# Both directions of a selective scan as one stage of 256 units instead of two stages of 128

## The chip, the cores and the metric

One core of one Trainium2 chip runs the whole layer in one launch. The metric is the device time of the program in microseconds (us), the median of several runs. One further execution was profiled; all rows below come from it.

## The reference, cut to what matters

The layer takes x as 1024 channels by 4096 pixels in float32. A first part (normalisation, a scan over channels) makes tokens `t`, 4096 of them with 1024 features. The second part is a bidirectional state space block on the normalised tokens. In it only the order of the sequence differs between the directions; each has weights of its own.

```python
def _direction(x_bdl, conv_w, conv_b, xproj_w, dtproj_w, dtproj_b, A_log, Dv):
    xc = depthwise_conv(x_bdl, conv_w, 4 taps, causal) + conv_b       # 2048 channels
    x_dbl = xc @ xproj_w.T                                            # 64 + 16 + 16 columns
    dt = x_dbl[..., :64] @ dtproj_w.T + dtproj_b
    Bm, Cm = x_dbl[..., 64:80], x_dbl[..., 80:]
    xc, dt = clip(xc, -10, 10), clip(dt, 1e-05, 1.0)
    delta = softplus(dt + dtproj_b);  A = -exp(A_log)
    # for each of 2048 channels and 16 states n, over 4096 tokens:
    #   h = exp(delta * A[n]) * h + (delta * xc) * Bm[n];   y += h * Cm[n]
    return y + xc * Dv
xz = (hidden_states @ in_proj_w.T).transpose(0, 2, 1);  x, z = split(xz)
y = (_direction(x, forward weights) + _direction(x[:, :, ::-1], backward weights)[:, ::-1]) * silu(z)
out = y @ out_proj_w.T
```

## The kernel before, in words

**Tiling.** Channels come in 16 blocks of 128 (`DB`), one channel to a partition, tokens in 8 chunks of 512 (`NCH`, `T`). A *unit* is one block of one chunk with its 16 states; `stage_scan` runs 128 units (`NU`), chunk after chunk, and is called twice: first with `rev=True` (tiles named `bwd_...`), then with `rev=False` (`fwd_...`). `flip` reverses the access patterns of the scan in the backward stage. A `Scope` ends with its semaphores cleared and a barrier of all engines.

**One unit, by engine.** For each state n, ScalarE (ACT) computes `da` = exp(delta * A[n]) into one of two PSUM buffers (L1027), VectorE (DVE) scans (L1171) and, for 12 of the 16 states (`VN`), multiplies by C (`weigh`, L1181). GpSimd (POOL) makes `w` = (delta * u) * B for four states at a time (`weigh_b`, L1122) and multiplies the other four states (`PN`) by C (`weigh_c`, L1131). TensorE (PE) transposes and sums the results in `yT` (L927, L894). ACT's order is fixed: at every n a `save` of a state, which waits for a scan (L1006), then `da`, then whatever hangs at that n.

**Work for later units.** Inside unit b, the input of unit a = b + 17 is prepared (`inputs_of`): in the backward stage the input projection (8 matmuls in two halves at n = 0 and 2, `in_step`), in both stages the convolution (4 diagonal matmuls at n = 5, `conv_step`, L822), ACT's `xc_copy` of it at n = 10 (L977), and the x projection (`project_step`). The forward stage reads the x that the backward one stored (`x_pad`) and instead projects z of its own unit (`in_step(b)`, `in_copy` at n = 7). The last 16 units of a stage have no later unit to prepare. The first chunk of a stage is prepared by `before_scan` in a loop ahead of all units, and `between` loads what the first units need.

**The chunk boundary.** B and C of a chunk (16 x 512 each) are a row product of all 16 blocks; they go to DRAM (`store_bc`) and come back to all 128 partitions by broadcast, 4 states at a time (`broadcast(k, c, g)`: c = 0 for B, 1 for C; L680; 1 MB of SBUF each). In the last unit of a chunk (`at == DB - 1`) the SP queue, which issues every DMA in the order of the code, does this: store of B and C; in the forward stage a hold on the last input matmul and then the 2 MB reload of `hn` (L648); store of `y_out`; B groups 0, 1, 2; C 0; B 3; store of `xc`; C 1; store of z. After a hold on all stores so far come the loads for the next units and, in the next unit, C 2 and 3. The backward stage reloads `hn` one unit earlier, since its input projections run 17 units ahead.

Of the kernel before, what the change touches and what calls it, by code (L numbers as in the profile page):

```python
# [9 lines left out]
P = 128  # L10
# [4 lines left out]
KT = C // P  # L15
# [10 lines left out]
G = 4  # L26
# [512 lines left out]
def stage_scan(nc, rev, ident, hnT_d, win_d, wx_d, wdt_d, convp_d, par_d, skip_d,  # L539
               x_pad_d, xc_d, z_d, bc_d, yT_d):  # L540
    name = "bwd" if rev else "fwd"


    first = rev
    with Scope(nc, name) as sc:
# [12 lines left out]
        par, skip = sc.sb("par", [P, DB, 1 + NS]), sc.sb("skip", [P, DB])  # L558
        convp = sc.sb("convp", [P, DB, TAPS + 1])
        prm = sc.sb("prm", [P, DB, NPAR])  # L560
        wdt = sc.sb("wdt", [R, 2, P])
        xc = sc.sb("xc", [P, 2, T])
        state = sc.sb("state", [P, DB * NS])
# [23 lines left out]
        NU = NCH * DB  # L587
# [4 lines left out]
        def t0(k):  # L592

            return (NCH - 1) * T - k * T if rev else k * T

        def col(k):
            return t0(k) + HALO

        def flip(ap):
            return ap[:, ::-1] if rev else ap  # L600

        last_col = 0 if rev else T - 1
# [6 lines left out]
        def state_of(b, n):  # L609
            i = (b % DB) * NS + n  # L610
            return state[:, i:i + 1]

        def decay(b, n):
            return prm[:, b % DB, n:n + 1]

        x_at = 0 if rev else HALO
        tap_at = [HALO - k if rev else k for k in range(TAPS)]
# [10 lines left out]

        POOL_AT = [5, 8, 11, 14]
        SKIP, DT_AT = 11, 13  # L630

        def stores_of(b):
            return 1 + len(inputs_of(b)) * (2 if first else 1) + (0 if first else 1)

        def stored_to(b):

            return (DB * (2 if first else 1) + sum(stores_of(i) for i in range(b + 1))) * LOAD
# [5 lines left out]
        def _(sp):  # L643
            def load_win(s, db):
                sp.dma_start(win[:, s], win_d[ds(db, 1)].rearrange("o p k d -> (o p) k d")).then_inc(win_in[s], LOAD)

            def load_hn(k):
                sp.dma_start(hn[:], hnT_d.rearrange("(k p) t -> p k t", p=P)[:, :, ds(t0(k), T)]  # L648
                             ).then_inc(S["hn_loaded"], LOAD)

            def load_a(s, db, k):

                if first:
                    halo = x[:, s, T:T + HALO]
                    sp.dma_start(halo, x_pad_d[ds(db * P, P), ds(col(k) + T, HALO)]).then_inc(a_in[s], LOAD)
                else:
                    sp.dma_start(x[:, s], x_pad_d[ds(db * P, P), ds(t0(k), T + HALO)]).then_inc(a_in[s], LOAD)
                sp.dma_start(wx[:, s], wx_d[ds(db, 1)].rearrange("o p k -> (o p) k")).then_inc(a_in[s], LOAD)

            def load_p(b):  # L660
                sp.dma_start(wdt[:, b % 2], wdt_d[b % DB]).then_inc(p_in[b % 2], LOAD)
                sp.dma_start(xc[:, b % 2], xc_d[b]).then_inc(p_in[b % 2], LOAD)

            def store_bc(k):

                hold(sp, S["proj_copied"], k + 1, S["passed"])
                sp.dma_start(bc_d[k], proj[R:XO, :]).then_inc(S["bc_stored"], LOAD)

            def broadcast(k, c, g):

                b = k * DB - 1
                if k and c == 0:
                    hold(sp, S["w_done"], b * NS + g * G + G, S["passed"])
                elif k:
# [3 lines left out]
                dst, sem = ((bcast_b, b_loaded), (bcast_c, c_loaded))[c]  # L678
                src = bc_d[k:k + 1, c * NS + g * G:c * NS + (g + 1) * G].rearrange("o n t -> (o n) t")
                sp.dma_start(dst[:, g * G:(g + 1) * G], src.partition_broadcast(P)).then_inc(sem[g], LOAD)  # L680

            def store_x(a):
                if first:
                    hold(sp, S["in_copied"], a + 3, S["passed"])
                    sp.dma_start(x_pad_d[ds(a % DB * P, P), ds(col(a // DB), T)],
                                 x[:, a % 2, x_at:x_at + T]).then_inc(S["stored"], LOAD)

            def store_xc(a):
                hold(sp, S["xc_copied"], a + 3, S["passed"])
                sp.dma_start(xc_d[a], xc_out[:, a % 2]).then_inc(S["stored"], LOAD)  # L690

            def before_scan(j, end=False):

                n = 2 if first else 1
                for s in range(2):
                    if first and not end:
                        hold(sp, S["in_mm"], j * 2 + s + 1, S["passed"])
                        load_win(s, j * 2 + s + 2)
                for s in range(2):
                    db = j * 2 + s  # L700
                    if first:
                        hold(sp, S["in_copied"], db + 3, S["passed"])
                        sp.dma_start(x_pad_d[ds(db * P, P), ds(col(0), T)],
                                     x[:, s, x_at:x_at + T]).then_inc(S["stored"], LOAD)
                    hold(sp, S["xc_copied"], db + 3, S["passed"])
                    sp.dma_start(xc_d[ds(db, 1)].rearrange("o p k -> (o p) k"),
                                 xc_out[:, s]).then_inc(S["stored"], LOAD)
                    hold(sp, S["stored"], j * (2 * n * LOAD) + (s + 1) * n * LOAD, S["passed"])
                    hold(sp, S["proj_mm"], db + 1, S["passed"])

            def between():
# [3 lines left out]
                if first:  # L715
                    for s in range(2):
                        load_win(s, s)
# [3 lines left out]
                if first:  # L721
                    load_hn(1)
                for s in range(2):
                    load_a(s, s, 1)
                if not first:
                    load_hn(0)
                    for s in range(2):
                        load_win(s, s)
# [3 lines left out]
            def unit(b):  # L732
                k, at = b // DB, b % DB
                more = k + 1 < NCH
                if at == 0 and b:
                    broadcast(k, 1, 2)
                    broadcast(k, 1, 3)
# [4 lines left out]
                if at == DB - 1 and more:  # L742
                    store_bc(k + 1)
                    if not first:
# [6 lines left out]
                if at == DB - 1 and more:  # L751
                    hold(sp, S["bc_stored"], (k + 2) * LOAD, S["passed"])
                    for g in range(3):
                        broadcast(k + 1, 0, g)
                for a, _ in inputs_of(b):
                    store_x(a)
                    if first and a % DB == DB - 1 and a + 1 < NU:
# [3 lines left out]
                if at == DB - 1 and more:  # L761
                    broadcast(k + 1, 1, 0)
                    broadcast(k + 1, 0, 3)
                for a, _ in inputs_of(b):
                    store_xc(a)
                if at == DB - 1 and more:
                    broadcast(k + 1, 1, 1)
                if not first:
                    hold(sp, S["in_copied"], b + 3, S["passed"])
                    sp.dma_start(z_d[ds(at * P, P), ds(t0(k), T)], z_out[:, b % 2]).then_inc(S["stored"], LOAD)  # L770

                hold(sp, S["stored"], stored_to(b), S["passed"])
                for a, _ in inputs_of(b):
                    hold(sp, S["proj_mm"], a + 1, S["passed"])
                    if a + 2 < NU:
                        if first:
                            load_win(a % 2, (a + 2) % DB)
                        load_a(a % 2, (a + 2) % DB, (a + 2) // DB)
                if not first and b + 2 < NU:
                    load_win(b % 2, (b + 2) % DB)  # L780

            sp.dma_start(par[:], par_d.rearrange("u p k -> p u k")).then_inc(S["par_loaded"], LOAD)
            sp.dma_start(convp[:], convp_d.rearrange("u p k -> p u k")).then_inc(S["par_loaded"], LOAD)
            if first:
                load_hn(0)
                for s in range(2):
                    load_win(s, s)
            for s in range(2):
                load_a(s, s, 0)
            for db in range(DB):  # L790
                sp.dma_start(skip[:, db:db + 1], skip_d[db]).then_inc(S["skip_loaded"], LOAD)
            with sp.Fori(0, DB // 2 - 1) as j:
                before_scan(j)
                for s in range(2):
                    load_a(s, j * 2 + s + 2, 0)
            before_scan(DB // 2 - 1, end=True)
# [4 lines left out]
            sp.dma_start(yT_d[NU], y_out[:, 1]).then_inc(S["stored"], LOAD)  # L801
# [4 lines left out]
        def _(pe):  # L806
# [13 lines left out]
            def convolution(s, bank=dt_ps[:]):  # L820
# [615 lines left out]
```

## Time and profile before

| | us |
|---|---|
| median of 3 runs (8814.04 to 8827.7) | 8817.02 |
| the profiled execution, own time | 8824.44 |
| its span in the trace | 8822.7 |
| DVE busy in the span | 7549.8 (86%) |
| PE busy | 7257.8 (82%) |
| POOL busy | 6819.9 (77%) |
| ACT busy | 4939.5 (56%) |

Times in the trace count from the start of the span. The backward stage fills about 626 to 4197, the forward one 4199 to 7767. What lies ahead is the first part of the layer, what follows is `stage_out`. A row of the timeline may merge several instructions of one form (x2, x16); its duration is then that of all of them, from the first start to the last end.

### The profile page before, as it was taken

The page shows a single profiled execution, that of the slowest core. Times are in us where ns is not written, and L with a number is a line of the kernel's source. Part 1 is how long each engine was busy: PE and PEld are TensorE (multiplying, and loading weights), DVE is VectorE, ACT ScalarE, POOL GpSimd, SP SyncE. Part 2 cuts the span into 40 slices and gives each one's busy share as a digit, 9 for nine tenths or more (in the row PEclk, how much of TensorE's full clock was granted, in tenths as well). Part 3 has the DMA queues.
Part 4 walks back from the last instruction along what each step waited for, and adds up shares of the span by engine and source line. Part 5 has one row for each costly group of instructions (what it writes and reads, how often), then busy time and mean ns, then how long its engine had stood idle before and what let it go on. Part 6 is the DMA issues. An engine that isn't in the chain of part 4 may idle for free. (4 is left out here: it accounts for less than half of the span.)

```text
span 8822.7 us, 108252 instructions
## 1 busy us (share of the span) xinstructions
PE 7257.8 (82%) x28624; PEld 4150.8 (47%) x28624; DVE 7549.8 (86%) x8367; ACT 4939.5 (56%) x11727; POOL 6819.9 (77%) x3031
## 2 busy tenths in 40 slices
PE   7458888888888888855688888888888887769999
PEld 3243555454555544444255445554555454434444
DVE  7940999999999999999199999999999999944444
ACT  3552666666666666665266666666666665610000
POOL 1211999999999999999299999999999999931110
PEclk9679999999999999966799999999999998879999
DMA  3263231313132313110323232323232322144442
GB/s 86 57 185 129 70 111 65 111 66 111 65 112 66 111 64 112 61 62 18 116 73 120 75 121 77 118 73 119 76 118 77 121 73 102 49 160 137 135 142 80
DMA packets 540929, 843.59 MB, mean 96 GB/s; under 512 B 112592, under 2 KB 260048, under 8 KB 522960
## 3 DMA queue, kind: packets, MB, share of 16 engines
q1 hardware_dynamic: 540368, 837.29, 28.7%
q8 instruction: 207, 3.39, 0.2%
q14 instruction: 354, 2.90, 0.1%
HBM read 583.83 MB, written 253.28 MB: 95 GB/s over the span
## 5 line engine op out<-in xcount | busy, mean ns | idle before, releaser
L1122 POOL TENSOR_TENSOR fwd_w<-fwd_du,fwd_bcast_b 128x2048 f32<-128x2048 f32 x511 | 2315.5, 4544 | 60.2 <-DMA fwd_bcast_b<-bc 60.2
L1122 POOL TENSOR_TENSOR bwd_w<-bwd_du,bwd_bcast_b 128x2048 f32<-128x2048 f32 x511 | 2316.4, 4545 | 4.0 <-DMA bwd_bcast_b<-bc 4.0
L1171 DVE TENSOR_TENSOR_SCAN bwd_h<-bwd_da,bwd_state,bwd_w 128x512 f32<-128x512 f32 x1536 | 1927.3, 1326 | 21.3 <-issue 14.0
L1171 DVE TENSOR_TENSOR_SCAN fwd_h<-fwd_da,fwd_state,fwd_w 128x512 f32<-128x512 f32 x1536 | 1921.0, 1318 | 26.0 <-POOL fwd_w L1122 10.6
L927 PE MATMUL bwd_yT<-all_ident,bwd_hc 128*128 128x128 f32 x6144 | 1021.6, 305 | 574.0 <-DVE bwd_hc L1181 566.1
L927 PE MATMUL fwd_yT<-all_ident,fwd_hc 128*128 128x128 f32 x6144 | 1000.4, 301 | 494.7 <-DVE fwd_hc L1181 486.7
L1027 ACT ACTIVATE fwd_da<-fwd_delta,fwd_prm 128x512 f32<-128x512 f32 x2048 | 1402.2, 685 | 0.0
L1027 ACT ACTIVATE bwd_da<-bwd_delta,bwd_prm 128x512 f32<-128x512 f32 x2048 | 1402.0, 685 | 0.0
L927 PEld LDWEIGHTS bwd_yT<-all_ident,bwd_hc 128*128 128x128 f32 x6144 | 748.2, 153 | 1061.5 <-DVE bwd_hc L1181 949.3
L927 PEld LDWEIGHTS fwd_yT<-all_ident,fwd_hc 128*128 128x128 f32 x6144 | 734.6, 151 | 985.4 <-DVE fwd_hc L1181 863.3
L1181 DVE TENSOR_TENSOR bwd_hc<-bwd_h,bwd_bcast_c 128x512 f32<-128x512 f32 x1536 | 1011.3, 726 | 16.7 <-ACT bwd_state L1006 16.7
L1181 DVE TENSOR_TENSOR fwd_hc<-fwd_h,fwd_bcast_c 128x512 f32<-128x512 f32 x1536 | 1005.5, 718 | 16.3 <-ACT fwd_state L1006 16.3
L816 PE MATMUL fwd_in_ps<-fwd_hn,fwd_win 128*128 128x512 f32 x2048 | 944.0, 604 | 16.8 <-DMA fwd_win<-winz 16.8
L1317 PE MATMUL out_o_ps<-out_yg,out_wout 128*128 128x512 f32 x2048 | 890.9, 594 | 0.0
L816 PE MATMUL bwd_in_ps<-bwd_hn,bwd_win 128*128 128x512 f32 x1792 | 811.2, 595 | 14.3 <-issue 14.3
L1006 ACT ACTIVATE bwd_state<-bwd_h 128x1 f32<-128x1 f32 x1536 | 259.4, 169 | 904.9 <-DVE bwd_h L1171 903.9
L1006 ACT ACTIVATE fwd_state<-fwd_h 128x1 f32<-128x1 f32 x1536 | 259.5, 169 | 895.6 <-DVE fwd_h L1171 894.7
L1286 POOL TENSOR_TENSOR out_yf<-out_yf,out_yb 128x512 f32<-128x512 f32 x128 | 162.7, 1271 | 755.2 <-DMA out_z<-z 755.2
L1171 DVE TENSOR_TENSOR_SCAN fwd_hs<-fwd_da,fwd_state,fwd_w 128x512 f32<-128x512 f32 x512 | 666.6, 1302 | 45.8 <-ACT fwd_da L1027 45.7
L1131 POOL TENSOR_TENSOR bwd_hp<-bwd_hs,bwd_bcast_c 128x512 f32<-128x512 f32 x512 | 656.3, 1282 | 28.2 <-issue 8.5
L1131 POOL TENSOR_TENSOR fwd_hp<-fwd_hs,fwd_bcast_c 128x512 f32<-128x512 f32 x512 | 655.7, 1281 | 27.7 <-issue 8.8
L1171 DVE TENSOR_TENSOR_SCAN bwd_hs<-bwd_da,bwd_state,bwd_w 128x512 f32<-128x512 f32 x512 | 670.7, 1310 | 3.7 <-ACT bwd_da L1027 3.5
(180 smaller groups left out, 9865.8 us busy)
## 6 DMA issues: line engine op xcount, KB each, us to landing
bwd_win<-winx SPq DMA_DIRECT2D x128, 512.0 KB, 3.5
fwd_win<-winz SPq DMA_DIRECT2D x128, 512.0 KB, 4.7
yT<-bwd_y_out SPq DMA_DIRECT2D x129, 256.0 KB, 2.0
yT<-fwd_y_out SPq DMA_DIRECT2D x129, 256.0 KB, 2.0
fwd_x<-x_pad SPq DMA_DIRECT2D x128, 257.5 KB, 2.8
n_xin<-x SPq DMA_DIRECT2D x64, 512.0 KB, 4.2
x_pad<-bwd_x SPq DMA_DIRECT2D x128, 256.0 KB, 3.0
xc<-bwd_xc_out SPq DMA_DIRECT2D x128, 256.0 KB, 2.0
```

Source lines behind the costliest of these rows:

```text
L816: last = nc.tensor.matmul(bank, win[:, s, i], hn[:, i], start=(i == 0), stop=(i == KT - 1))
L927: last = nc.tensor.matmul(yT[:, tb], hc[:, i % NOUT, tb * P:(tb + 1) * P], ident[:], is_transpose=True, start=(i == 0 and tb == 0), stop=( ...
L1006: nc.scalar.activation(state_of(unit_, n_), h_slot(n_)[:, last_col:last_col + 1], ACT.Copy).then_inc(S["h_saved"], 1)
L1027: nc.scalar.activation(da[:, n % 2], delta[:, s], ACT.Exp, scale=decay(b, n)).then_inc(S["exp_done"], 1)
L1122: nc.gpsimd.tensor_tensor(w[:, g], du[:, s].unsqueeze(1).to_broadcast([P, G, T]), bcast_b[:, g * G:(g + 1) * G], ALU.mult).then_inc(S["w_d ...
L1131: nc.gpsimd.tensor_tensor(hp[:, i], hs[:, i], bcast_c[:, n], ALU.mult).then_inc(S["hp_done"], 1)
L1171: nc.vector.tensor_tensor_scan(flip(h_slot(n)), flip(da[:, n % 2]), flip(w[:, n // G, n % G]), state_of(b, n), ALU.mult, ALU.add).then_inc ...
L1181: nc.vector.tensor_tensor(hc[:, i % NOUT], h_slot(n), bcast_c[:, n], ALU.mult).then_inc(S["hc_done"], 1)
L1286: nc.gpsimd.tensor_tensor(yf[:, s], yf[:, s], yb[:, s], ALU.add).then_inc(summed, 1)
L1317: last = nc.tensor.matmul(o_ps[:, q % 2], wout[:, q, b], yg[:, g, b], start=(b == 0), stop=(b == DB - 1))
```

## The change

One stage named `scan` has `NU` = 256 units; units 0 to 127 are the backward ones (`back`). Chunk numbers run from 0 to 15, and `t0`, `flip`, `decay`, `state_of` choose by direction. Tables of parameters and states hold both directions. The tile `mag` goes: its two steps work in place in `v`. `ud` has one buffer instead of two, with a wait on `yT_copied`. There is no second setup, `before_scan` and `between`; `inputs_of` now gives units 111 to 127 an input too, a forward one without input projection. SP's order in the last unit of a forward chunk changes. The weights of the prologue are loaded in another order.

```diff
-def stage_scan(nc, rev, ident, hnT_d, win_d, ...
+def stage_scan(nc, ident, hnT_d, winx_d, winz_d, ...
-        mag = sc.sb("mag", [P, T])
-        delta, u, du, ud = (sc.sb(n, [P, 2, T]) for n in ("delta", "u", "du", "ud"))
+        delta, u, du = (sc.sb(n, [P, 2, T]) for n in ("delta", "u", "du"))
+        ud = sc.sb("ud", [P, T])
+        HALF = NCH * DB
+        NU = 2 * HALF
+        def back(i):
+            return i % NU < HALF
+        def in_steps_of(b):
+            if not back(b):
+                return [(b, NORMAL)]
+            return [(a, when) for a, when in inputs_of(b) if back(a)]
...
+            def before_scan(a):
+                store_x(a)
+                store_xc(a)
+                hold(sp, S["stored"], (a + 1) * 2 * LOAD, S["passed"])
+                hold(sp, S["proj_mm"], a + 1, S["passed"])
+                load_a(a + 2)
...
             def between():
                 for b in range(2):
                     load_p(b)
                 store_bc(0)
-                if first:
-                    for s in range(2):
-                        load_win(s, s)
+                for a in range(2):
+                    load_win(DB + a)
                 hold(sp, S["bc_stored"], LOAD, S["passed"])
                 for c, g in ((0, 0), (0, 1), (1, 0)):
                     broadcast(0, c, g)
-                if first:
-                    load_hn(1)
-                for s in range(2):
-                    load_a(s, s, 1)
...
+                load_hn(1)
                 for c, g in ((0, 2), (1, 1), (0, 3), (1, 2), (1, 3)):
                     broadcast(0, c, g)
...
                 if at == DB - 1 and more:
-                    store_bc(k + 1)
-                    if not first:
-                        hold(sp, S["in_mm"], b + 1, S["passed"])
-                        load_hn(k + 1)
-                hold(sp, S["yT_copied"], b + 1, S["passed"])
-                sp.dma_start(yT_d[b], y_out[:, (b + 1) % 2]).then_inc(S["stored"], LOAD)
+                    store_bc(chunk + 1)
+                hold(sp, S["yT_copied"], b + 1, S["passed"])
+                sp.dma_start(yT_d[direction(b - 1)][(b - 1) % HALF + 1 if b else 0],
+                             y_out[:, (b + 1) % 2]).then_inc(S["stored"], LOAD)
                 if at == DB - 1 and more:
-                    hold(sp, S["bc_stored"], (k + 2) * LOAD, S["passed"])
-                    for g in range(3):
-                        broadcast(k + 1, 0, g)
+                    hold(sp, S["bc_stored"], (chunk + 2) * LOAD, S["passed"])
+                    for g in range(2):
+                        broadcast(chunk + 1, 0, g)
+                    if not back(b):
+                        hold(sp, S["in_mm"], b + 1, S["passed"])
+                        load_hn(chunk + 1)
+                    broadcast(chunk + 1, 0, 2)
...
+            for d in range(2):
+                i = (1 - d) * DB
+                sp.dma_start(par[:, i:i + DB], par_d[d].rearrange("u p k -> p u k")).then_inc(S["par_loaded"], LOAD)
+                sp.dma_start(convp[:, i:i + DB], convp_d[d].rearrange("u p k -> p u k")).then_inc(S["par_loaded"], LOAD)
+            load_hn(0)
+            for a in range(2):
+                load_win(a)
+                load_a(a)
+            for d in range(2):
+                for db in range(DB):
+                    i = (1 - d) * DB + db
+                    sp.dma_start(skip[:, i:i + 1], skip_d[d][db]).then_inc(S["skip_loaded"], LOAD)
...
                     if n == 10:
-                        act.wait_ge(S["skip_loaded"], DB * LOAD)
+                        act.wait_ge(S["skip_loaded"], 2 * DB * LOAD)
                         act.wait_ge(S["u_done"], b + 1)
-                        nc.scalar.activation(ud[:, s], u[:, s], ACT.Copy,
-                                             scale=skip[:, b % DB:b % DB + 1]).then_inc(S["ud_done"], 1)
+                        act.wait_ge(S["yT_copied"], b + 1)
+                        nc.scalar.activation(ud[:], u[:, s], ACT.Copy,
+                                             scale=skip[:, block_of(b):block_of(b) + 1]).then_inc(S["ud_done"], 1)
...
-        for rev in (True, False):
-            d = int(rev)
-            stage_scan(nc, rev, ident, hnT, winx if rev else winz, wx[d], wdt[d], convp[d], par[d], skip[d], x_pad, xc, z, bc,
-                       yT[d])
+        stage_scan(nc, ident, hnT, winx, winz, wx, wdt, convp, par, skip, x_pad, xc, z, bc, yT)
```

## Rows read from the trace of the kernel before

**Rows 1.** The page's first part: busy us of each engine, share of the span, instructions.
```profile
PE 7257.8 (82%) x28624; PEld 4150.8 (47%) x28624; DVE 7549.8 (86%) x8367; ACT 4939.5 (56%) x11727; POOL 6819.9 (77%) x3031
```
**Rows 2.** Two stretches: length; busy PE, PEld, DVE, ACT, POOL; PEclk, DMA share, GB/s.
```profile
1150.67:1566.35 415.68, 360.65 (x1541) 210.68 (x1540) 415.68 (x449) 283.67 (x706) 407.81 (x177) 0.95 0.26 89
3806.00:4168.00 362.00, 210.56 (x970) 165.25 (x970) 362.00 (x392) 217.19 (x531) 356.09 (x155) 0.66 0.06 21
```
**Rows 3.** Timeline of DVE: start us, us, instruction, [idle before it]; first scans of some units.
```profile
889.64 2.46 DVE L1171 TENSOR_TENSOR_SCAN bwd_h<-bwd_da,bwd_state,bwd_w 128x512 f32<-128x512 f32 x2
...
4168.41 2.55 DVE L1171 TENSOR_TENSOR_SCAN bwd_h<-bwd_da,bwd_state,bwd_w 128x512 f32<-128x512 f32 x2
...
4357.15 2.51 DVE L1171 TENSOR_TENSOR_SCAN fwd_h<-fwd_da,fwd_state,fwd_w 128x512 f32<-128x512 f32 x2 [10.07 <-issue]
...
4403.88 2.46 DVE L1171 TENSOR_TENSOR_SCAN fwd_h<-fwd_da,fwd_state,fwd_w 128x512 f32<-128x512 f32 x2
...
4767.56 2.56 DVE L1171 TENSOR_TENSOR_SCAN fwd_h<-fwd_da,fwd_state,fwd_w 128x512 f32<-128x512 f32 x2
...
7738.93 1.30 DVE L1171 TENSOR_TENSOR_SCAN fwd_h<-fwd_da,fwd_state,fwd_w 128x512 f32<-128x512 f32 x1
```
**Rows 4.** Waits, 4390 to 7766 (forward): total us, times, longest us.
```profile
ACT fwd_mag L955 <- POOL fwd_v L1099: 51.6, 35, 5.8
POOL fwd_w L1122 <- DMA fwd_bcast_b<-bc: 51.3, 7, 7.8
DVE fwd_hs L1171 <- ACT fwd_da L1027: 45.2, 15, 5.0
```
**Rows 5.** The same view, 890 to 4168 (backward): DVE's longest entry.
```profile
DVE bwd_hs L1171 <- ACT bwd_da L1027: 3.5, 3, 1.5
```
**Rows 6.** Timeline of SP at the first forward boundary: issues.
```profile
4766.89 0.36 SPq L667 DMA_DIRECT2D bc<-fwd_proj  x1
4777.55 0.38 SPq L648 DMA_DIRECT2D fwd_hn<-hnT  x1
...
4778.74 3.17 SPq L680 DMA_DIRECT2D fwd_bcast_b<-bc  x3
```
**Rows 7.** DMA issues there: count, KB each, median us to landing.
```profile
fwd_hn<-hnT SPq DMA_DIRECT2D x1, 2048.0 KB, 9.9
...
fwd_bcast_b<-bc SPq DMA_DIRECT2D x1, 1024.0 KB, 11.8
```
**Rows 8.** Timeline of POOL at the same boundary.
```profile
4790.76 4.53 POOL L1122 TENSOR_TENSOR fwd_w<-fwd_du,fwd_bcast_b 128x2048 f32<-128x2048 f32 x1 [6.87 <-DMA fwd_bcast_b<-bc]
```
**Rows 9.** Timeline of PE: two groups of transposes; four of convolutions, two after idle time.
```profile
3865.67 1.97 PE L927 MATMUL bwd_yT<-all_ident,bwd_hc 128*128 128x128 f32 x8 [2.75 <-DVE bwd_hc L1181]
...
4782.04 1.03 PE L927 MATMUL fwd_yT<-all_ident,fwd_hc 128*128 128x128 f32 x8
...
1161.19 3.60 PE L822 MATMUL bwd_dt_ps<-bwd_x,bwd_diag 128*128 128x512 f32 x8
...
700.52 7.03 PE L822 MATMUL bwd_da<-bwd_x,bwd_diag 128*128 128x512 f32 x16
...
4207.93 10.14 PE L822 MATMUL fwd_da<-fwd_x,fwd_diag 128*128 128x512 f32 x16 [5.89 <-ACT fwd_diag L998]
...
4244.94 8.70 PE L822 MATMUL fwd_da<-fwd_x,fwd_diag 128*128 128x512 f32 x16 [7.13 <-ACT fwd_diag L998]
```
**Rows 10.** Timeline of ACT around the convolution's copy, unit 10.
```profile
1139.13 0.67 ACT L977 ACTIVATE bwd_xc_out<-bwd_dt_ps,bwd_convp 128x512 f32<-128x512 f32 x1
1140.18 0.17 ACT L1006 ACTIVATE bwd_state<-bwd_h 128x1 f32<-128x1 f32 x1 [0.37 <-DVE bwd_h L1171]
```
**Rows 11.** Timeline of SP in the backward prologue.
```profile
626.63 0.96 SPq L783 DMA_DIRECT2D bwd_convp<-convp  x1
...
633.16 10.76 SPq L791 DMA_DIRECT2D bwd_skip<-skip  x16
```
**Rows 12.** The page's group of POOL's B products, backward: idle before them at the end.
```profile
L1122 POOL TENSOR_TENSOR bwd_w<-bwd_du,bwd_bcast_b 128x2048 f32<-128x2048 f32 x511 | 2316.4, 4545 | 4.0 <-DMA bwd_bcast_b<-bc 4.0
```

More of the change, by code:

```diff
@@ L529, in _, with stage_scan @@
                 sp.wait_ge(hn_stored[s], (NT // 2 + 1) * LOAD)
-def stage_scan(nc, rev, ident, hnT_d, win_d, wx_d, wdt_d, convp_d, par_d, skip_d,
+def stage_scan(nc, ident, hnT_d, winx_d, winz_d, wx_d, wdt_d, convp_d, par_d, skip_d,
                x_pad_d, xc_d, z_d, bc_d, yT_d):
-    name = "bwd" if rev else "fwd"
-    first = rev
-    with Scope(nc, name) as sc:
+    with Scope(nc, "scan") as sc:
         hn = sc.sb("hn", [P, KT, T])
@@ L632, in stores_of @@
         def stores_of(b):
-            return 1 + len(inputs_of(b)) * (2 if first else 1) + (0 if first else 1)
+            return 1 + sum(2 if back(a) else 1 for a, _ in inputs_of(b)) + (0 if back(b) else 1)
         def stored_to(b):
-            return (DB * (2 if first else 1) + sum(stores_of(i) for i in range(b + 1))) * LOAD
+            return (2 * DB + sum(stores_of(i) for i in range(b + 1))) * LOAD
         block = sc.block()
@@ L660, in load_p @@
             def load_p(b):
[L661 to L672, printed above, removed]
+                sp.dma_start(wdt[:, b % 2], wdt_d[direction(b)][b % DB]).then_inc(p_in[b % 2], LOAD)
@@ L673, in broadcast, with store_bc @@
+                sp.dma_start(xc[:, b % 2], xc_d[b % HALF]).then_inc(p_in[b % 2], LOAD)
+            def store_bc(chunk):
+                hold(sp, S["proj_copied"], chunk + 1, S["passed"])
+                sp.dma_start(bc_d[chunk % NCH], proj[R:XO, :]).then_inc(S["bc_stored"], LOAD)
+            def broadcast(chunk, c, g):
+                b = chunk * DB - 1
+                if chunk and c == 0:
                     hold(sp, S["w_done"], b * NS + g * G + G, S["passed"])
-                elif k:
+                elif chunk:
@@ L732, in unit @@
             def unit(b):
-                k, at = b // DB, b % DB
-                more = k + 1 < NCH
+                chunk, at = b // DB, b % DB
+                more = b + DB < NU
                 if at == 0 and b:
-                    broadcast(k, 1, 2)
-                    broadcast(k, 1, 3)
+                    broadcast(chunk, 1, 2)
+                    broadcast(chunk, 1, 3)
                 if b + 2 < NU:
@@ L775, in unit @@
                     if a + 2 < NU:
[L776 to L796, printed above, removed]
+                        if back(a + 2):
+                            load_win(a + 2)
+                        load_a(a + 2)
+                if HALF <= b + 2 < NU:
+                    load_win(b + 2)
+            for d in range(2):
[10 more added lines that the diff above has]
+                    sp.dma_start(skip[:, i:i + 1], skip_d[d][db]).then_inc(S["skip_loaded"], LOAD)
+            for j in range(DB // 2):
+                for a in (j * 2, j * 2 + 1):
+                    if a + 2 < DB:
+                        hold(sp, S["in_mm"], a + 1, S["passed"])
+                        load_win(a + 2)
+                for a in (j * 2, j * 2 + 1):
+                    before_scan(a)
             between()
@@ L907, in unit @@
                         dt_matmul(b + 2)
-                    for a, when in ins if first else [(b, NORMAL)]:
+                    for i, when in in_steps_of(b):
                         if n in when["into"]:
-                            in_step(a, when["into"].index(n))
+                            in_step(i, when["into"].index(n))
                     for a, when in ins:
```

165 lines of the change are left out of this document (70 added, 95 removed).

## The prediction

> **What bounds the kernel now.** I read the page's busy shares first, then the stretches, then DVE's timeline at the borders of units, then the waits, and last the single boundaries. The shares [rows 1] name DVE, but only with 86%. The first stretch shows where it is everything: 16 units (11 to 26) take 415.68 us and DVE is busy for all of them [rows 2], so a unit is 415.68 / 16 = 25.98 us of DVE work. POOL is close behind, 407.81 / 16 = 25.49 us. The second stretch, the last backward chunk, has no inputs to prepare; DVE is again busy for 362.00 of 362.00 us. With or without preparation a unit is DVE's 25.98, at least while TensorE's clock is high: in that second stretch the granted clock is 0.66, between its levels of 1.2 and 2.4 GHz, against 0.95 [rows 2].
>
> So time can only be lost where DVE stands still: between the stages, in a stage's first unit, and at chunk boundaries. DVE's timeline prices all three [rows 3]. The last backward unit starts at 4168.41, the first forward one at 4357.15. The first forward unit runs until 4403.88. From there to the start of the last unit (7738.93) lie 126 units; 126 x 25.98 = 3273.5, and they take 3335.0. The backward stage needs from 889.64 to 4168.41, 3278.8, for the same 126.
>
> **The change, term by term.** The sum is made against the profiled execution, 8824.44 us (span 8822.7), which lies 7.4 above the median of 8817.02; the difference is carried over to the median.
>
> (A) *No second prologue.* The gap 4357.15 - 4168.41 = 188.7 becomes one unit, 25.98: **-162.8**. It holds the end of the scope, setup, eight rounds of `before_scan` and `between`. Their matmuls and ACT work don't vanish, they move into units 111 to 127; (E) prices that.
>
> (B) *No second first unit.* 4403.88 - 4357.15 = 46.7 becomes 25.98: **-20.8**. Unit 128 prepares one input, not two, and everything it reads was loaded in units 110 to 127 (its `hn` chunk in unit 110, z's weights in 126).
>
> (C) *B ahead of hn.* The seven forward boundaries cost 3335.0 - 3273.5 = 61.5 [rows 3]. The seven backward ones cost 3278.8 - 3273.5 = 5.3, unit 1's share included. Why the forward ones cost more is seen in the waits: POOL waits 51.3 us in 7 times for B's broadcast, ACT 51.6 for POOL's `v` behind it, DVE 45.2 for `da` behind that [rows 4]; in the backward stage DVE's longest entry is 3.5 [rows 5]. At the first boundary SP stores B and C at 4766.89, then stands on the hold until 4777.55, issues `hn`, and only then the B groups at 4778.74 [rows 6]. `hn` lands after 9.9 us, the first B group after 11.8, at 4790.5 [rows 7], and POOL starts at 4790.76 after 6.87 of waiting [rows 8]; it wanted it at 4783.9. In the new order the store of `y_out` and B groups 0 and 1 are issued as soon as the store of B and C has landed, about 4771 (my estimate: 4 us after 4766.89). Even at 11.8 us they land at 4783, and with no `hn` ahead of them earlier. The hold moves behind them but ends at the same moment, so queued behind it stand `hn`, B 2, C 0, B 3, `xc`, C 1 and z, none later than now, with 2 MB less in front. `hn` lands at about 4787.5 as now; the input projection wants it some 2 us into the next unit, 4767.56 + 25.98 + 2 = 4795.5 [rows 3]. What is late next: SP's hold on all stores, then C 2 and 3. They too move forward, by about 5 us (two broadcasts). So I expect the forward boundaries to look like backward ones, 5.3 / 7 = 0.76 each. Eight boundaries at that price (the new one, 127 to 128, has no `hn` in it) are 6.1: 61.5 - 6.1 = **-55.4**. Bounds: nothing gained, or all 61.5.
>
> (D) *The first prologue.* SP issues a second pair of tables ahead of `hn`; one `convp` takes 0.96 us to issue [rows 11], the pair about 1.4, and its small pieces occupy the queues as long again: +1.4 to +3. 16 more `skip` loads take at most another 10.76 us of SP, which now ends at about 656 instead of 644; the next thing in SP's queue is the weight load for block 2, wanted by PE at about 664 and landing 4 us after issue, so the cover holds by some 4 us, and costs what is missing if it doesn't. The loop itself is PE's and doesn't shorten. After it, the last `load_a` (two issues, 1.1 us) now stands ahead of `load_p`, which the first `dt` matmul waits for: +1.1. Against this, B group 2 is no longer queued behind 8 us of `load_a`; POOL waited 4.0 us for it in the whole stage [rows 12], so at best -4. I take **+4**, bounds -3 and +9.
>
> (E) *Preparation in units 112 to 127.* Regular units hide it, but at a high clock. There the convolution starts 1161.19 - 1150.67 = 10.5 us into the unit, lasts 3.60 and ends at 14.1 [rows 9]. ACT's copy starts at 14.4 (1139.13 in a unit begun at 1124.69) and the next `save` then has 0.37 us of idle time before it [rows 10]. So there is hardly any slack in ACT's order: if the convolution ends later, ACT waits at its place and `da` for the next scan is late. How much DVE forgives is bounded by rows 10 (0.37) and by the longest wait of ACT for `v`, 5.8, of which DVE felt 5.0 [rows 4]: 0.4 to 0.8, I take 0.6. The new units lack the 7.2 us of input projection that keep PE busy before. Today PE idles 2.75 us before the transposes at 9.0 us into unit 115, and these 8 take 1.97 us where 8 others take 1.03: 1.2 GHz against 2.4 [rows 9]. The convolution will follow right on such transposes. What a start at 1.2 GHz costs is shown by groups of 16 that began after idle time: 10.14 and 8.70 us, against 7.03 for one on a busy PE [rows 9]; the eight of the forward prologue have a mean of 9.28, a loss of 2.25, within 1.7 to 3.1. From transposes to the end of the convolution nearly all of that is lost too. 2.25 - 0.6 = 1.65 a unit, and I count 14 of 16 units: **+23**. Bounds: 0 (the clock stays up), and 64 if all of it runs at 1.2 GHz: 3.6 more for 8 passes, 1.0 more for the transposes, less 0.6, by 16.
>
> The Trainium skill, "TensorE: Matmul & The Clock Gate", section "HAM oscillation — how this bites in real kernels", says that a PE whose bursts are separated by waits is throttled again each time and starts every burst slow. By it all 16 units pay, 1.65 x 16 = 26; were it wrong here, the term would be 0 and the forecast 8581. The 0.66 above agrees with it.
>
> (F) *Priced at nothing.* `mag` in `v`: each writer of `v` already follows the last reader in ACT's order. One `ud`: PE reads it at n = 11, ACT writes the next at n = 10 of the next unit; the new wait is on a copy made at n = 2 of the same unit. Behind it in ACT stand `xc_copy` and the `da` of n = 11, so a late one would hit DVE directly, but 8 states lie between. Loads of x for forward inputs (257 KB instead of 1.5) run a unit ahead of need in a stretch with a DMA share of 0.06 [rows 2]. `stage_out` is untouched.
>
> Sum: -162.8 - 20.8 - 55.4 + 4 + 23 = -212.0. The profiled execution would be 8612.4, the median **8605**.
>
> **Rivals.**
> 1. *The clock is no matter*: it stays up, or ACT doesn't notice. For it: units with a z projection in the last forward chunk hold 25.98. Against it: they have PE work right at the start, these have none. 8605 - 23 = 8582.
> 2. *Convolutions wholly at 1.2 GHz*: (E) is 64, 8646. Against it: no group of 16 stayed low to its end.
> 3. *The boundary wait changes its place*, so that (C) doesn't do what it says: C 1 to 3 or z's stores, behind 6.5 MB issued within 7 us, become the late ones. For it: `hn` still shares the stretch with the broadcasts. Against it: none is later than today, and DVE doesn't wait for C now. Half of (C) lost: 8633.
> 4. *Slower than before*: POOL, with 25.49 of 25.98 us busy, becomes the bound because all tiles of the stage get new places and its products run longer. It has 0.49 us of slack a unit; to eat the 212 us it needs 212 / 256 = 0.83 more, so it decides from 1.3 us or 5% of its work. At 7% it would be 1.29 us a unit beyond the slack, 331 us: 8936. Against it: both stages, with different tiles around, have the same product time within 1 ns in the page's groups.
>
> **How the numbers follow.** Forecast 0.58; rival 1 0.21; rival 2 0.08; rival 3 0.10; rival 4 0.02; the remaining 0.01 is a loss that just cancels the gain. The forecast's own spread is (D) and (E) within their nearer bounds, about +-15. The range 8572 to 8648 runs from rival 1 with the best of (D) and (C) to rival 2 and leaves some 0.12 outside. A measurement here tells about 0.2% (18 us) from no change. Faster 0.97, within 0.2% 0.01, slower 0.02.
>
> **What would show it.** (A) and (B): DVE's first forward scan 26 to 28 us after that of unit 127, and unit 128 no longer than 28. (C): POOL's wait for B under 5 us in the forward half. (D): first scan at 841 to 846 instead of 839. (E): units 112 to 127 at 27 to 28 us, ACT's wait for the convolution in them 2 us each, clock 0.7 to 0.8; units at 25.98 prove rival 1. The prediction is wrong if regular units leave 25.98 or if (E) passes 45.

## The result, and the profile after

| | before | after |
|---|---|---|
| median of four runs each, side by side | 8815.53 us (8813.94 to 8827.7) | 8613.05 us (8609.99 to 8615.87) |
| profiled execution (its span) | 8824.44 (8822.7) | 8615.87 (8614.1) |
| mean granted clock | 0.908 | 0.916 |

The ratio is 0.9767, with a 95% interval of 0.975 to 0.9784. Forecast was 8605, in a range of 8572 to 8648. Between the medians lie 202.5 us. Between the profiled executions, on which the forecast's sum of 212.0 was made, lie 208.6.

The page of after, shares of the busy time and two rows of its 40 slices (tenths):

```profile
PE 7207.2 (84%) x28624; PEld 4128.4 (48%) x28624; DVE 7548.3 (88%) x8364; ACT 4928.4 (57%) x11720; POOL 6814.0 (79%) x3026
...
DVE  7940999999999999999999999999999999934443
PEclk9679999999999999987899999999999998879999
```

Against [rows 1] DVE's work is the same, within 1.5 us; what is gone is standing still. Behind the prologue no slice of DVE in the scan stage is under 9 any more: the hole in the middle has closed, and the dip of TensorE's granted clock there is left (8, 7, 8). DVE's timeline, start and duration of the scans with which units begin, prices every term:

```profile
843.88 1.29 DVE L1163 TENSOR_TENSOR_SCAN scan_h<-scan_da,scan_state,scan_w 128x512 f32<-128x512 f32 x1 [14.49 <-issue]
...
3763.01 1.30 DVE L1163 TENSOR_TENSOR_SCAN scan_h<-scan_da,scan_state,scan_w 128x512 f32<-128x512 f32 x1
...
4198.32 2.46 DVE L1163 TENSOR_TENSOR_SCAN scan_h<-scan_da,scan_state,scan_w 128x512 f32<-128x512 f32 x2
4225.63 2.46 DVE L1163 TENSOR_TENSOR_SCAN scan_h<-scan_da,scan_state,scan_w 128x512 f32<-128x512 f32 x2
4251.62 2.46 DVE L1163 TENSOR_TENSOR_SCAN scan_h<-scan_da,scan_state,scan_w 128x512 f32<-128x512 f32 x2
...
7530.47 2.47 DVE L1163 TENSOR_TENSOR_SCAN scan_h<-scan_da,scan_state,scan_w 128x512 f32<-128x512 f32 x2
```

They are the first scans of units 0, 111, 127, 128, 129 and 255. From unit 127 to 128 pass 27.31 us, where [rows 3] has 188.7; unit 128 lasts 25.99. From 129 to 255 pass 3278.85, that is 5.4 over 126 x 25.98 = 3273.5. Units 111 to 127 take 462.62, 21.0 more than 17 x 25.98.

The waits of after, 4240 to 7550 (the forward half), and then 3789 to 4226 (units 112 to 127): engine, tile and line, what it waited for, total us, times, longest.

```profile
ACT scan_v L948 <- POOL scan_v L1091: 21.7, 32, 1.2
...
DVE scan_hs L1163 <- ACT scan_da L1020: 4.2, 3, 3.2
```
```profile
ACT scan_xc_out L970 <- PE scan_dt_ps L819: 30.1, 16, 1.9
```

In the first, POOL's wait for B, 51.3 us in [rows 4], has no entry at all, and DVE's wait for `da` went from 45.2 to 4.2. The second is the new cost. One of its units (116, begun at 3898.00), first PE, then ACT:

```profile
3906.99 1.97 PE L920 MATMUL scan_yT<-all_ident,scan_hc 128*128 128x128 f32 x8 [2.75 <-DVE scan_hc L1173]
...
3909.60 4.74 PE L819 MATMUL scan_dt_ps<-scan_x,scan_diag 128*128 128x512 f32 x8
...
3914.44 0.69 ACT L970 ACTIVATE scan_xc_out<-scan_dt_ps,scan_convp 128x512 f32<-128x512 f32 x1 [1.91 <-PE scan_dt_ps L819]
```

The transposes run at 1.2 GHz (1.97 us, as the first row of [rows 9]), the convolution begins 11.6 us into the unit and ends after 16.34 (16.36 in most of the sixteen), where a regular unit has 14.12. ACT stands 1.91 us at its place. And a stretch of either kind, from the middle of unit 112 to that of unit 127, and 16 regular units: length; busy PE, PEld, DVE, ACT, POOL; clock, DMA share, GB/s.

```profile
3804.00:4213.00 409.00, 285.37 (x1203) 192.32 (x1202) 391.71 (x421) 256.63 (x647) 381.82 (x165) 0.75 0.17 54
1150.00:1566.00 416.00, 361.26 (x1543) 211.77 (x1543) 416.00 (x449) 283.92 (x706) 407.69 (x177) 0.94 0.26 90
```

DVE is busy for 391.71 of 409.00 us in the one and for all 416.00 in the other.

### The profile page after: what moved, and what is told of

It is laid out like the page before. It is cut to its first block and busy times, and to the rows that moved or that the text cites. A ratio compares the mean times of both kernels' runs of the same rounds, so it can differ in the third digit from the quotient of the medians.

```text
span 8614.1 us, 107712 instructions
## 1 busy us (share of the span) xinstructions
PE 7207.2 (84%) x28624; PEld 4128.4 (48%) x28624; DVE 7548.3 (88%) x8364; ACT 4928.4 (57%) x11720; POOL 6814.0 (79%) x3026
## 5 line engine op out<-in xcount | busy, mean ns | idle before, releaser
L1114 POOL TENSOR_TENSOR scan_w<-scan_du,scan_bcast_b 128x2048 f32<-128x2048 f32 x1023 | 4629.4, 4537 | 3.6 <-DMA scan_bcast_b<-bc 3.6
L1163 DVE TENSOR_TENSOR_SCAN scan_h<-scan_da,scan_state,scan_w 128x512 f32<-128x512 f32 x3072 | 3787.0, 1282 | 21.8 <-issue 14.5
L920 PE MATMUL scan_yT<-all_ident,scan_hc 128*128 128x128 f32 x12288 | 1992.4, 300 | 1010.9 <-DVE scan_hc L1173 995.5
L1020 ACT ACTIVATE scan_da<-scan_delta,scan_prm 128x512 f32<-128x512 f32 x4096 | 2803.6, 685 | 0.0
L920 PEld LDWEIGHTS scan_yT<-all_ident,scan_hc 128*128 128x128 f32 x12288 | 1466.6, 151 | 1974.6 <-DVE scan_hc L1173 1741.8
L1173 DVE TENSOR_TENSOR scan_hc<-scan_h,scan_bcast_c 128x512 f32<-128x512 f32 x3072 | 1955.5, 682 | 16.9 <-ACT scan_state L1000 16.9
L812 PE MATMUL scan_in_ps<-scan_hn,scan_win 128*128 128x512 f32 x3840 | 1741.0, 596 | 13.3 <-issue 13.3
L1123 POOL TENSOR_TENSOR scan_hp<-scan_hs,scan_bcast_c 128x512 f32<-128x512 f32 x1024 | 1306.5, 1276 | 73.7 <-issue 47.0
L1163 DVE TENSOR_TENSOR_SCAN scan_hs<-scan_da,scan_state,scan_w 128x512 f32<-128x512 f32 x1024 | 1297.5, 1267 | 32.1 <-ACT scan_da L1020 31.9
L819 PE MATMUL scan_dt_ps<-scan_x,scan_diag 128*128 128x512 f32 x1920 | 882.3, 602 | 0.0
```

The costliest lines, as they stand in the source:

```text
L812: last = nc.tensor.matmul(bank, win[:, s, i], hn[:, i], start=(i == 0), stop=(i == KT - 1))
L819: last = nc.tensor.matmul(bank, diag[:, s, i], x[:, s, at:at + T], start=(i == 0), stop=(i == TAPS - 1))
L920: last = nc.tensor.matmul(yT[:, tb], hc[:, i % NOUT, tb * P:(tb + 1) * P], ident[:], is_transpose=True, start=(i == 0 and tb == 0), stop=( ...
L1020: nc.scalar.activation(da[:, n % 2], delta[:, s], ACT.Exp, scale=decay(b, n)).then_inc(S["exp_done"], 1)
L1114: nc.gpsimd.tensor_tensor(w[:, g], du[:, s].unsqueeze(1).to_broadcast([P, G, T]), bcast_b[:, g * G:(g + 1) * G], ALU.mult).then_inc(S["w_d ...
L1123: nc.gpsimd.tensor_tensor(hp[:, i], hs[:, i], bcast_c[:, n], ALU.mult).then_inc(S["hp_done"], 1)
```

## The experiments

Each kernel ran three to five rounds beside the kernel before; its ratio is to that. The kernel before took 8815 to 8827 us beside them, so differences of a few us between experiments are read from traces, not from times.

**1. The new order of SP's queue alone, in two stages** (term C by itself, on the kernel before):

```diff
-                    if not first:
-                        hold(sp, S["in_mm"], b + 1, S["passed"])
-                        load_hn(k + 1)
...
-                    for g in range(3):
+                    for g in range(2):
...
+                    if not first:
+                        hold(sp, S["in_mm"], b + 1, S["passed"])
+                        load_hn(k + 1)
+                    broadcast(k + 1, 0, 2)
```

> The kernel before (two stages) with only SP's order in the last unit of a forward chunk changed: B groups 0 and 1 are issued ahead of the reload of hn. Theory (the waits at forward boundaries are SP's order alone): the seven forward boundaries fall from 61.5 us to about 5, POOL's waits for B from 51 us to under 5, and the time to about 8815 - 56 = 8759 (ratio 0.9936). Rival (what cured them is the single stage, its tiles or its phase): boundaries stay near 8.8 us each and the time stays within 10 us of 8815.

Measured: 8773.47 us (8769.02 to 8778.23), before 8820.93; ratio 0.9946 (0.993 to 0.9963), 47 us less. POOL's one wait for B left between 4240 and 7700 is that of the forward stage's first unit, at no boundary:

```profile
POOL fwd_w L1123 <- DMA fwd_bcast_b<-bc: 7.4, 1, 7.4
```

So the order by itself brings term C without the joined stage: by the traces the forward boundaries fall from 61.5 to 11.7 us, where the joined kernel has 5.4. Most of what is left are three jumps (1.6, 3.3 and 3.3 us) at which ACT waits for a slow z projection; they come back below.

**2. The reverse: the joined stage with the old order** (the hold and `load_hn` again ahead of the store of `y_out` and of B):

```diff
+                    if not back(b):
+                        hold(sp, S["in_mm"], b + 1, S["passed"])
+                        load_hn(chunk + 1)
...
-                    if not back(b):
-                        hold(sp, S["in_mm"], b + 1, S["passed"])
-                        load_hn(chunk + 1)
```

> The changed kernel with SP's old order in forward boundary units: hold on the input matmul and reload of hn ahead of the store of y_out and of all B groups. Theory (order alone): the boundaries after units 143 to 239 cost about 8.8 us each again, POOL waits about 50 us for B, time about 8613 + 56 = 8669 (0.9834 of before). Rival (the single stage cured them): about 8613. The border of the directions (unit 127 to 128) has no reload, so by both it stays as it is.

Measured: 8666.68 us (8665.92 to 8670.55), ratio 0.9828 (0.9811 to 0.9844), 53.6 more than after. Waits, 4240 to 7700:

```profile
POOL scan_w L1114 <- DMA scan_bcast_b<-bc: 50.8, 7, 8.0
...
ACT scan_v L948 <- POOL scan_v L1091: 51.0, 38, 4.8
...
DVE scan_hs L1163 <- ACT scan_da L1020: 40.5, 13, 4.3
```

These are nearly the waits of [rows 4], and the forward boundaries cost 58.3 us again. Two kernels, each with one part, add up to the whole: 47.5 us less by the order alone (experiment 1) and 154.3 less by all but the order (this one) make 201.7, against 202.5. It is the place of the reload and its hold in a queue. What isn't separated is the hold from the transfer. At the first forward boundary the first B group is issued 11.1 us into the unit and lands 11.5 us later, in after 3.8 and 4.4. The delay is 14.4 us, 7.3 of it by the hold and 7.1 by the transfers ahead, and POOL waits 6.6 of it; so either part alone might have cost next to nothing (an estimate; not run).

**3. PE kept busy in units 111 to 127.** Work is added: eight matmuls of zeros a unit, into a tile that nobody reads then. (A row's x8 is four matmuls of the code: the trace has 272 matmul records more for these 136.)

```diff
+if HALF - DB - 1 <= b < HALF and n in (0, 2):
+    if n == 0:
+        pe.wait_ge(S["in_copied"], HALF + 2)
+    for i in range(4):
+        nc.tensor.matmul(in_ps[:], zero[:, 0:P], zero[:], start=(i == 0), stop=(i == 3))
```

> The changed kernel with 4 + 4 matmuls of a zero tile into the free input bank at n = 0 and 2 of units 111 to 127, the place and number of the missing input projection. Their result is not read. Theory (those units are longer because the convolution starts at the lower clock): work is added and the time falls; the convolution starts 10.5 us into the unit and ends at 14.1, units 111 to 127 go from 26.5 to 27.3 back to 25.98, in all -21 us, about 8592. Rival (the added convolution, x projection and diagonals themselves are too much for PE or ACT, whatever the clock): units stay at 27.3 or grow, 8613 or more.

Measured: 8592.61 us (8592.34 to 8593.25), ratio 0.9742 (0.9726 to 0.9759): 20.4 us less than after, with 136 matmuls more. Units 111 to 126 last 25.98; unit 127, a boundary unit, lasts 28.82. The stretch 3804 to 4168, and PE in unit 116 (begun at 3886.36):

```profile
3804.00:4168.00 364.00, 315.87 (x1350) 183.82 (x1349) 364.00 (x393) 240.63 (x603) 358.28 (x156) 0.95 0.14 44
```
```profile
3886.99 3.60 PE L908 MATMUL scan_in_ps<-scan_zero 128*128 128x512 f32 x8
...
3896.86 3.60 PE L819 MATMUL scan_dt_ps<-scan_x,scan_diag 128*128 128x512 f32 x8
```

The clock is 0.95 instead of 0.75 and the convolution 3.60 us instead of 4.74, begun 10.5 us into the unit. The clock is the cause. Unit 127 shows it once more: its first four matmuls of zeros take 6.40 us, the convolution ends 17.9 us into the unit, and ACT waits 3.4 for it.

**4. The clock left low, ACT's copy of the convolution and PE's x projection two steps later**, in units 111 to 127 only:

```diff
+AHEAD = dict(into=(0, 2), diag=1, copy=7, conv=5, xc=12, proj=13)
...
+            if back(b) and not back(b + DB + 1):
+                return [(b + DB + 1, AHEAD)]
```

> The changed kernel; in units 111 to 127 ACT copies the convolution's result at n = 12 instead of 10 and PE takes the x projection at n = 13 instead of 11. The convolution and the clock stay as they are. Theory (the slow convolution costs time only through its fixed place in ACT's order): ACT doesn't wait for it any more and the units go to 25.98 though the convolution still ends 16.4 us into the unit; about 8592. Rival (DVE is held up by PE itself, through late transposes, or by something else in these units): units stay near 27.3, 8613.

Measured: 8587.92 us (8586.65 to 8596.0), ratio 0.9736 (0.972 to 0.9753). Same stretch, PE in unit 116 (begun at 3887.96), and ACT:

```profile
3804.00:4168.00 364.00, 243.66 (x1125) 163.93 (x1124) 364.00 (x394) 239.56 (x602) 357.97 (x157) 0.81 0.15 44
```
```profile
3899.56 4.18 PE L822 MATMUL scan_dt_ps<-scan_x,scan_diag 128*128 128x512 f32 x8
...
3905.29 0.68 ACT L973 ACTIVATE scan_xc_out<-scan_dt_ps,scan_convp 128x512 f32<-128x512 f32 x1
```

The convolution is again late (11.6 to 15.8 us into the unit), but nobody is waiting for it, and units 111 to 127 last 25.98. With experiment 3 this gives both halves of the cause: a low clock makes the matmuls late, and ACT's fixed order hands that to DVE. Either half removed removes the cost.

**5. `mag` and a second `ud` buffer restored** (term F; `ud` again `[P, 2, T]`, the `ln` and `exp` steps in `mag`, the wait for `yT_copied` gone):

```diff
+        mag = sc.sb("mag", [P, T])
-        delta, u, du = (sc.sb(n, [P, 2, T]) for n in ("delta", "u", "du"))
-        ud = sc.sb("ud", [P, T])
+        delta, u, du, ud = (sc.sb(n, [P, 2, T]) for n in ("delta", "u", "du", "ud"))
...
-                        act.wait_ge(S["yT_copied"], b + 1)
```

> The changed kernel with mag and the second buffer of ud restored, and the wait that one ud needs taken out again. Theory (both were priced at nothing): every unit keeps its length, 25.98 us and 27.3 in units 112 to 127, time 8613 within 6. Rival (the single buffers cost something in every unit or place the late copies): regular units shorter than 25.98, or units 112 to 127 below 27, time below 8605.

Measured: 8613.6 us (8610.53 to 8615.7), ratio 0.9763 (0.9748 to 0.9778), no difference from after. The saved memory is free.

**6. The first prologue** (term D): the forward tables are loaded behind `hn`, the first weights and inputs; the last `load_a` behind `load_p`.

```diff
-            for d in range(2):
+            def load_tables(d):
...
+            load_tables(1)
...
+            load_tables(0)
```

> The changed kernel with another order of loads ahead of the units: the forward tables after hn and the first weights instead of ahead of them, and the last load_a behind load_p. Theory (the first scan comes 4.7 us later than before, 843.9 against 839.2, through these two): first scan back at 839 to 841 us, time about 8609, which the comparison of medians can hardly tell, the trace can. Rival (it is the second set of skip loads, which stays): first scan stays at 843 to 844.

Measured: 8607.2 us (8606.88 to 8610.45), ratio 0.9756 (0.9741 to 0.9771). The first scan starts at 842.2, after's at 843.9. In experiments 7 to 10, which hold this edit too, it starts between 840.1 and 841.6, in those of the joined stage without it between 843.1 and 844.1: worth 1 to 4 us, 2.6 between the means.

**7. More slack everywhere.** Experiment 4's steps in all units, with PE's z projection copied at 9, beside experiment 6's order. Meant for the boundaries, which in after still cost some 16 us (10.7 backward, 5.4 forward).

```diff
-        NORMAL = dict(into=(0, 2), diag=1, copy=7, conv=5, xc=10, proj=11)
+        NORMAL = dict(into=(0, 2), diag=1, copy=7, conv=5, xc=12, proj=13)
+        Z = dict(into=(0, 2), copy=9)
```

> e_prologue's order, and later places in ACT's order for what waits for PE, in all units: copy of the convolution at n = 12 and x projection at n = 13, copy of z at n = 9 instead of 7. Theory (the jumps of 0.3 to 3.35 us at boundaries are the clock falling just when the input projection runs, felt only through the place of the copy in ACT's order): forward boundaries and the single 0.88 of unit 245 go to under 0.5 in sum, backward boundaries keep theirs (their copy at n = 7 stays), units 112 to 127 at 25.98; 8613 - 21 - 5 - 4, about 8583. Rival (the jumps are something else, as SP's queue or the broadcasts): about 8588 with jumps on both sides.

A miss: 8647.4 us (8643.27 to 8651.87), ratio 0.9803 (0.9789 to 0.9816), 40 us slower than experiment 6. The forward boundary units and units 112 to 127 are at 25.98, as expected. But every few other units, nearly all at 25.98 until then, now last 0.5 to 2.6 us more: units 1 to 110 lose 45.3 us against 110 x 25.98 (after: 10.7), units 129 to 254 lose 26.5 (after: 5.4). A regular stretch, and the waits of 900 to 4225:

```profile
1150.00:1566.00 416.00, 366.19 (x1522) 219.62 (x1521) 411.43 (x444) 278.73 (x699) 402.54 (x175) 0.90 0.27 89
```
```profile
ACT scan_y_out L993 <- PE scan_yT L927: 64.2, 41, 3.5
ACT scan_x L974 <- PE scan_in_ps L819: 63.3, 52, 1.7
```

The clock is 0.90 where after has 0.94, and two other waits of ACT for PE have come: between 900 and 3750 they are 63.9 us (39 times) for `y_out` and 62.8 (51) for x, where after has no such wait for `y_out` and 15.1 (7) for x. PE does the same work, placed otherwise. At unit 20 (begun at 1390.42, 27.64 long):

```profile
1387.49 2.07 PE L814 MATMUL scan_dt_ps<-scan_proj,scan_wdt 64*128 64x512 f32 x2
1389.49 2.02 PE L831 MATMUL scan_proj_ps<-scan_xc_out,scan_wx 128*96 128x512 f32 x2
...
1394.84 0.60 ACT L993 ACTIVATE scan_y_out<-scan_yT 128x512 f32<-128x512 f32 x1 [2.29 <-PE scan_yT L927]
```

The `dt` matmul takes 2.07 us where after's takes 1.12, and the x projection follows it at the same low clock across the border of the units; the next transposes are late, and ACT stands at `y_out`. In after that x projection is slow too (1.91 us), but it ends more than 3 us ahead of the border, and nobody waits. The low clock comes before the loss, in a unit that still lasts 25.98.

**8. The same, with still later steps in the last unit of backward chunks.**

```diff
+        BORDER = dict(into=(0, 2), diag=1, copy=9, conv=7, xc=13, proj=14)
...
+            when = BORDER if back(b + DB + 1) and (b + 1) % DB == 0 else NORMAL
```

> e_slack, and in the last unit of a backward chunk also the copy of the input projection at n = 9, convolution at 7, its copy at 13, x projection at 14. Theory: backward boundaries lose their jumps too (9 us in sum in the changed kernel), about 8576 if none is left. Rival: the later store of xc puts C group 1 behind it in SP's queue, 4 us later than now, and DVE waits for C instead: no gain or a few us more than e_slack.

Measured: 8641.81 us (8639.16 to 8643.72), ratio 0.9794 (0.9781 to 0.9808), a miss too: the same losses in regular units (39.6 and 27.8 us in the two stretches named).

**9. Experiments 4 and 6 together.**

> e_xc_later (later copy of the convolution in units 111 to 127 alone) with e_prologue's order of loads; regular units have their old places. The runs of e_slack had later places everywhere: units 112 to 127 and the boundaries lost their excess, but every few regular units gained 1.1 to 2 us. Theory (that came from moving PE's x projection in regular units, which moved where the clock falls): regular units stay at 25.98 here, and the time is that of e_xc_later less 2 to 3 us, about 8585. Rival (the loss came from e_prologue's loads or the tables' places): above 8595 with regular units of 27.

Measured: 8584.29 us (8581.57 to 8594.47, five runs), before 8827.12 (8820.01 to 8835.95); ratio 0.973 (0.9717 to 0.9743). Regular units are at 25.98, the first scan at 840.14. It beats before and after; from experiment 4 (0.9736) it can't be told.

**10. Experiment 9, with the later steps also in the last unit of each forward chunk.**

```diff
+            if not back(b) and (b + 1) % DB == 0 and b + DB + 1 < NU:
+                return [(b + DB + 1, AHEAD)]
...
+                return [(b, dict(into=(0, 2), copy=9) if (b + 1) % DB == 0 else NORMAL)]
```

> e_both, and in the last unit of each forward chunk alone also: copy of z at n = 9, copy of the convolution at 12, x projection at 13. Theory (a boundary jump is ACT standing at its place for a slow input projection): the jumps after forward boundaries (4 to 7 us in sum in the changed kernel) go, the backward ones stay, about 8580. Rival (moving the places moves the fall of the clock, as in e_slack): new losses of 1 to 2 us in units next to the boundaries, no gain.

Measured: 8589.78 us (8582.6 to 8590.54), ratio 0.9729 (0.9716 to 0.9743). The forward boundary units are at 25.98, where experiment 9 has jumps of 3.3, 0.7 and 0.4 us. Instead unit 144, next to a boundary, is 2.54 us longer (ACT waits 3.1 us for the store of z) and unit 177 0.66. So the rival was right in part, and no gain over experiment 9 can be told. Few units so changed leave the regular ones at 25.98, unlike experiment 7.

## Why the prediction was right, and where it was off

| term | forecast | measured in the traces |
|---|---|---|
| (A) no second prologue | -162.8 | -162.8 (27.31 for 188.7; 1.33 of it counted in E) |
| (B) no second first unit | -20.8 | -20.8 |
| (C) forward boundaries | -55.4 | -56.1 (5.4 left of 61.5; 11.7 in experiment 1) |
| (D) first prologue | +4 | +4.7 |
| (E) units 111 to 127 | +23 | +20.9 (21.0; 0.1 before) |
| (F) buffers | 0 | 0 |
| backward boundaries (units 1 to 110) | not in it | +5.5 |
| sum | -212.0 | -208.6 (whole executions: -208.6) |

(A), (B): right; read from one view, they needed no theory.

(C): right in mechanism and size, shown from both sides by experiments 1 and 2, though no experiment took the hold and the transfer apart. Rival 3, a transfer further back that becomes late, falls: `hn` moved behind 2 MB of B, and POOL's longest wait for C is 0.7 us.

(D): right in sum, its parts less so. `hn` is issued at 631.14 and was at 627.64. Of these 3.5 us 0.5 lie before the stage's first load (626.67 and 626.19), so the tables cost 3.0, the upper end of my 1.4 to 3. PE's first projections start 3.3 us later and take 16.96 us instead of 16.09, which the sum lacked; `load_a` ahead of `load_p` cost 1.3 more, and 0.8 came back before the first scan. The cover over the skip loads held: the weights for block 2 land at 657.6 and PE takes them at 668.4. SP after the change:

```profile
631.14 1.57 SPq L656 DMA_DIRECT2D scan_hn<-hnT  x1
...
636.56 17.39 SPq L785 DMA_DIRECT2D scan_skip<-skip  x32
654.06 6.07 SPq L653 DMA_DIRECT2D scan_win<-winx  x2
```

(E): the mechanism was right and two sizes were off against each other. The convolution ended 2.2 us late (forecast 2.25) and ACT waited 1.9 (forecast 2). DVE forgave about 0.9, not 0.6 and outside my 0.4 to 0.8, so that a unit pays 1.33 and not 1.65; and all 16 pay, not 14. 16 x 1.33 = 21.3, against 21.0 measured. That +23 came so close is in part luck. The number of units is where the Trainium skill ("TensorE: Matmul & The Clock Gate", section "HAM oscillation — how this bites in real kernels") was nearer than my 14 of 16: by it, every burst behind a long enough wait starts slow. The trace agrees: in every unit of the sixteen PE stands 2.75 us or more before the transposes, and the convolution takes 4.37 to 4.77 us instead of 3.60. Rivals 1 and 2 fall, and experiments 3 and 4 show that the clock and ACT's order are each necessary.

Rival 4 fell too: POOL's product of B takes 4537 ns in after's page, 4545 in [rows 12].

```profile
L1114 POOL TENSOR_TENSOR scan_w<-scan_du,scan_bcast_b 128x2048 f32<-128x2048 f32 x1023 | 4629.4, 4537 | 3.6 <-DMA scan_bcast_b<-bc 3.6
```

What the sum lacked is the last row. I had taken the backward boundaries for unchanged, since their code is. Units 1 to 110 cost 10.7 us over 110 x 25.98 instead of 5.2, mainly by jumps of 3.35 us in units 31 and 79 and of 1.65 in unit 47. Unit 31 (begun at 1675.29) lasts 29.33; PE, then ACT and DVE:

```profile
1677.94 6.19 PE L812 MATMUL scan_in_ps<-scan_hn,scan_win 128*128 128x512 f32 x8
1684.84 3.60 PE L812 MATMUL scan_in_ps<-scan_hn,scan_win 128*128 128x512 f32 x8
```
```profile
1688.53 0.60 ACT L967 ACTIVATE scan_x<-scan_in_ps 128x512 f32<-128x512 f32 x1 [4.06 <-PE scan_in_ps L812]
...
1690.42 1.28 DVE L1163 TENSOR_TENSOR_SCAN scan_hs<-scan_da,scan_state,scan_w 128x512 f32<-128x512 f32 x1 [3.21 <-ACT scan_da L1020]
```

The first half of that projection takes 6.19 us and the second 3.60: again a low clock, again a wait of ACT in its order. Which boundaries are hit isn't set by the code there. Experiments 2, 3 and 4 change nothing that runs before unit 111, and yet the larger jumps are in units 31, 47 and 79 in after, 63 and 79 in experiment 2, 47 and 95 in experiment 3, 47 in experiment 4. In all ten traced kernels whose units 1 to 110 have the old places, these units cost between 2.3 (experiment 5) and 10.7 us (after), so the traced execution of after was the unluckiest. One execution of each was traced; that one kernel varies so from execution to execution is likely but not shown. Why the clock is low at one boundary and not at the next stays open. By these rows it is the mechanism of (E), met by chance, and a spread of about -3 to +6 us against before should have stood for it in the sum. The forward boundaries have it too: with the new order they cost from 3.9 (experiment 10) to 11.7 us (experiment 1), so that (C)'s -56.1 is near the lucky end.

Of experiment 7's moves, z's copy isn't needed for the loss: the backward units project no z, and their clock fell (0.94 to 0.90) and they lost most. It was the later copy of the convolution with the x projection behind it; these two weren't run apart.

The range's ends don't quite follow from the terms: rival 1 with the best of (D) and (C) is 8582 - 7 - 6 = 8569, not 8572, and rival 2 is 8646, not 8648. The measured time lies inside either.

## What to carry to other kernels

A transfer that can wait may stand between a busy engine and the one it waits for: look at what each hold in a DMA queue keeps behind it before the sizes of the transfers, and try the order first. Where TensorE has little to do, the clock it then gets can still cost time, by way of another engine that waits for it in a fixed order; give that copy a later place in just the units concerned, and leave the units alone in which the clock is high. Price a boundary with a spread, since whether a low clock meets it changes even where its code doesn't.

## What the runs showed of the hardware

- Added matmuls of zeros made the kernel faster: 8592.6 us against 8613.05, since the granted clock of the stretch went from 0.75 to 0.95.
- The x projection two steps later in all units took the clock of a regular stretch from 0.94 to 0.90; with z's copy moved too this cost 40 us (8647.4 against 8607.2). Slack for a late matmul isn't free if it changes when PE works.
- Whether a boundary unit meets the low clock isn't set by its code: units 1 to 110, the same in after and experiments 2 to 4, cost 10.7, 5.8, 5.3 and 6.1 us over their 25.98 each.
- 32 loads of `skip` took SP 17.39 us to issue, 0.54 each, where 16 took 10.76 [rows 11]: twice the loads cost 1.6 times.
